# One attention's weights used as fp32 instead of a split pair, in a two-block kernel on one core

## The chip, the core and the metric

The kernel runs on one core of a Trainium2 chip. The core has a matrix engine (TensorE, PE in the profile), a vector engine (VectorE, DVE), an activation engine (ScalarE, ACT), a general engine (GpSimd, POOL) and a queue engine that only starts transfers here (SyncE, SP). Each works through its own list of instructions in order, and they meet through semaphores. The metric is the device time of one execution in microseconds.

## The reference

Sixteen images of 32 x 32 pixels and 128 channels go through two blocks, all in fp32:

```
perceived = depthwise 3x3 conv(x)              # 3 maps per channel
h   = x + up2(gelu(up1(perceived)))            # 128 -> 384 -> 256 -> 128 channels
y   = h + local_attention(h)                   # 3x3 window, softmax over 9
xn  = group_norm(y, 8 groups)
s   = (xn Wq + bq) (xn Wk + bk)^T * scale      # 1024 x 1024 per image
out = xn + (softmax(s) (xn Wv + bv)) Wp + bp
```

The change touches the last product, softmax(s) times the values.

## The kernel before, in words

An image is 1024 pixels, or eight tiles of 128 queries (`TILES`). Most products on TensorE are made of fp32r operands split in two: ScalarE rounds an operand to a high part, a second engine subtracts to get the low part, and `mm3` (L571 to L578) issues three matmuls, high by low, low by high and high by high (L576, L577, L578).

The program is software-pipelined over images by hand. Each engine has three lists of calls: `fill_program`, `turn_program(it)` and `drain_program`. `run` executes the fill, one turn for `it` = 1, a hardware loop of turns for `it` = 2 to 12, and the drain: 12 turns in all. In a turn the names are z = it-1, a = it, b = it+1, c = it+2, d = it+3: a turn finishes the last attention of image a, does the local attention and group norm of image b and the convolution of image c. The order of the calls within a list is the order on the engine. The products use four PSUM banks (`work`); `BANK_PLAN`, `FILL_PLAN` and `DRAIN_PLAN` name for each use its bank, and a product waits (`bank_free`) until the previous user of its bank has been read.

The last attention of an image runs like this, for tile t of eight:

- `scores(n, t)`: TensorE writes 128 x 1024 scores into `ps_s` or `ps_t`; `row_max` (VectorE, L1990) takes the maximum, `exp` (ScalarE, L1116) writes the exponentials `e` and their sums; two `e` buffers.
- `turn_e` (VectorE, L1997) transposes 32 x 32 blocks into `turned`; `send` (SP, L433) writes that to memory (`spread`); `fetch` (SP, L448) reads it back in four transfers as tile t of `et_f`, so that keys lie on partitions. `et_f` holds four tiles, t modulo 4, and `fetch` waits until `values` has read the tile that was there.
- `et_hi_tile` (ScalarE, L1121) rounds the tile to `et_hi`; `et_lo_tile` (GpSimd, L1508) subtracts to get `et_lo`.
- The value operand is the turned xn: `vv` (TensorE), `vv_hi_half` (ScalarE, L1108), `vv_lo_half` (VectorE, L1983).
- `values(n, j)` multiplies two tiles at once: eight key tiles with `mm3`, 24 matmuls of 256 columns into one bank. `a_part` (ScalarE, L1127) copies the result, `attended` (TensorE, L704) applies Wv Wp, `output` (VectorE, L2009) scales and adds `r_tok`, which `residual` (GpSimd, L1567 and L1570) makes from `vv_hi + vv_lo` and then `bp_row`.

Other work that the prediction speaks of: the convolution's six products `conv(c, k)`; their combination on VectorE (`sum_and_difference` L1851, `combine` L1858, `combine_own` L1865, `end_row` L1873); `gelu` and `g_hi_part` on ScalarE (L1029, L1034), `g_lo_part` on GpSimd, then `up2(c, 0)` on TensorE; the transform of the next image (`transform_ends` L1762); the moments and the group norm (`channel_moments` L1943, `group_norm` L1959).

Of the kernel before, what the change touches and what calls it, by code (L numbers as in the profile page):

```python
# [31 lines left out]
F32 = mybir.dt.float32  # L32
F32R = mybir.dt.float32r
# [24 lines left out]
class Count:  # L58
# [14 lines left out]
    ("vv", 1, 0, 1), ("pv", 3, -1, 2), ("pj", 1, -1, 2), ("conv", 0, 2, 0), ("at", 1, 1, 2), ("as", 3, 1, 3),  # L73
    ("conv", 1, 2, 3), ("conv", 2, 2, 1), ("conv", 3, 2, 2), ("at", 2, 1, 3), ("conv", 4, 2, 1), ("at", 3, 1, 2),
# [5 lines left out]
]  # L80
FILL_PLAN = [
    ("conv", 0, 0, 2), ("conv", 1, 0, 0), ("conv", 2, 0, 1), ("conv", 3, 0, 3), ("conv", 4, 0, 2), ("conv", 5, 0, 0),
    ("conv", 0, 1, 3), ("conv", 1, 1, 1), ("conv", 2, 1, 3), ("conv", 3, 1, 0), ("up2", 0, 0, 1), ("conv", 4, 1, 3),
# [15 lines left out]
    ("pv", 3, 12, 2), ("as", 3, 14, 1), ("vv", 1, 13, 2), ("pj", 1, 12, 0), ("conv", 0, 15, 3), ("conv", 1, 15, 0),  # L99
    ("conv", 2, 15, 2), ("conv", 3, 15, 3), ("at", 1, 14, 0), ("conv", 4, 15, 2), ("at", 2, 14, 3),  # L100
# [48 lines left out]
def conv_seq_kernel(nc, ins, out):  # L149
    ctx = ExitStack()  # L150
    with ctx:
# [13 lines left out]
        def placed(name, shape, offset, dt=F32):  # L165
# [65 lines left out]
        vv_at = region("vv_mem", 2 * TILES * 128)  # L231
        vv_hi, vv_lo = (placed(f"vv_{p}", [128, TILES, 128], vv_at + 4 * TILES * 128 * k, F32R)
                        for k, p in enumerate(("hi", "lo")))
# [8 lines left out]
        et_hi, et_lo = (placed(f"et_{p}", [128, 4, 4, TILES, 32], et_at + 4 * TILES * HALF * k, F32R)  # L242
                        for k, p in enumerate(("hi", "lo")))
        et_f = placed("et_f", [128, 4, 4, TILES, 32], et_at + 4 * TILES * HALF)
# [23 lines left out]
        def score_tile(n, t):  # L268
# [32 lines left out]
        vv_hi_ready, vv_lo_ready = count("vv_hi_ready", 2), count("vv_lo_ready", 2)  # L301
        v_sum_ready, r_tok_ready = count("v_sum_ready", 2), count("r_tok_ready", 2)
        max1_ready, e_ready, e_turned, et_hi_ready, et_lo_ready = (
            count("max1_ready", 8), count("e_ready", 8), count("e_turned", 8), count("et_hi_ready", 8),
            count("et_lo_ready", 8))
# [20 lines left out]
                        vv=vv_lo_ready, pv=a_ready, pj=o_ready)  # L326
# [80 lines left out]
        def _(sp):  # L407
# [28 lines left out]
            def fetch(n, t):  # L436

                landed, read = e_sent[t % 2].after(n, t // 2), pe["pv"].after(n, t // 2 - 2)
# [8 lines left out]
                for i in range(4):  # L447
                    sp.dma_start(et_f[32 * i:32 * (i + 1), t % 4].rearrange("r s k q -> r s (k q)"),  # L448
                                 spread[t % 4, :, i].rearrange("(s r) c -> r s c", s=4)) \
                      .then_inc(e_fetched[t % 4].handle, 16)  # L450
# [6 lines left out]
            def fill_program():  # L457
                load_x(1)
                load_x(2)
                send(0, 0)  # L460
                load_x(3)
# [5 lines left out]
                send(0, 4)  # L467
                fetch(0, 2)
                fetch(0, 3)
                send(0, 5)  # L470
                fetch(0, 4)
                fetch(0, 5)

# [3 lines left out]
            def turn_program(it):  # L477
                z, a, d = it - 1, it, it + 3
                send(z, 6)
# [3 lines left out]
                store(z, 0)  # L483
                load_x(d)
                send(a, 0)
                send(a, 2)
                send(a, 1)
                fetch(a, 0)
                fetch(a, 2)
                store(z, 1)  # L490
                fetch(a, 1)
                send(a, 3)
                fetch(a, 3)
                send(a, 5)
# [1885 lines left out]
```

## Time and profile before

| | |
|---|---|
| median of 3 runs | 1090.01 us (1089.63 to 1095.34) |
| profiled execution, own time | 1094.47 us |
| its span, first to last instruction | 1092.7 us |
| mean granted TensorE clock | 0.961 |
| busy: PE, DVE, ACT, POOL | 959.8, 924.5, 727.5, 716.3 us |

A busy share says how long an engine had an instruction in flight, not how long it was needed. Matmuls overlap, so their durations do not add up; the distance between two starts is what one costs in a stream. A wait is put down to the instruction that released it. The granted clock of a stretch is given as a share of 2.4 GHz.

### The profile page before, as it was taken

The numbers are of one execution on the slowest core, as the hardware profiler recorded it, in microseconds if no ns is written. First come the engines' busy times: TensorE is split into PE (matmuls) and PEld (weight loads), VectorE is DVE, ScalarE is ACT, GpSimd is POOL, SyncE is SP. The second block draws the span as 40 slices with busy tenths as digits, with TensorE's granted clock in tenths as the row PEclk, the third lists the DMA queues.
The fourth block names the chain that finished last, engine by engine and source line by source line (L and its number), as shares of the span: only waits on it lengthen the run. The fifth ranks groups of instructions, "written<-read, shape, count | busy, mean of one in ns | idle before, by whom it ended". The sixth has DMA issues, their size and how long they took to land.

```text
span 1092.7 us, 20391 instructions
## 1 busy us (share of the span) xinstructions
PE 959.8 (88%) x6036; PEld 862.8 (79%) x6036; DVE 924.5 (85%) x1628; ACT 727.5 (67%) x1379; POOL 716.3 (66%) x493
## 2 busy tenths in 40 slices
PE   5979898998888999888898988899888898989885
PEld 4968788787787888778797787888778788878775
DVE  6768898888989888898988889888898988987771
ACT  3466876676757767676666767767676676777662
POOL 3644685867667676776767566676775867665665
PEclk9999999999999999999999999999999999999897
DMA  5103465653655546355653655556355554545774
GB/s 89 21 1 85 134 159 169 155 150 101 173 161 123 153 151 169 103 142 168 141 163 115 147 159 126 144 158 169 96 153 164 134 163 132 149 144 154 209 232 138
DMA packets 177654, 152.88 MB, mean 140 GB/s; under 512 B 77776, under 2 KB 161104, under 8 KB 177616
## 3 DMA queue, kind: packets, MB, share of 16 engines
q1 hardware_dynamic: 176768, 152.03, 51.3%
q10 hardware_dynamic: 848, 0.39, 0.2%
q8 instruction: 19, 0.31, 0.1%
q14 instruction: 19, 0.16, 0.0%
HBM read 76.87 MB, written 75.50 MB: 139 GB/s over the span
## 4 chain that ended last, share of the span: by engine, by line
PE 45%; issue 15%; DVE 15%; POOL 4%; DMA 3%; SPq 2%; ACT 1%; DVEq 0%; ACTq 0%; POOLq 0%
PE work L576 9%; PE work L578 9%; PE work L577 9%; DVE turned L1997 3%; PE work L635 2%; DMA spread<-turned 2%; SPq L448 2%; PE ps_s L576 2%; PE work L669 2%; DVE nm L1990 2%; POOL et_lo L1508 2%; DVE gn L1959 2%; PE ps_t L576 2%; PE ps_t L577 2%; PE ps_t L578 2%
## 5 line engine op out<-in xcount | busy, mean ns | idle before, releaser
L1508 POOL TENSOR_TENSOR et_lo<-et_f,et_hi 128x1024 fp32r<-128x1024 f32 x128 | 319.2, 2501 | 129.5 <-ACT et_hi L1121 129.4
L1121 ACT ACTIVATE et_hi<-et_f 128x1024 fp32r<-128x1024 f32 x128 | 135.0, 1057 | 130.5 <-DMA et_f<-spread 130.5
L576 PE MATMUL work<-et_lo,vv_hi 128*128 128x256 f32 x512 | 158.4, 309 | 41.0 <-DVE u L1873 32.9
L576 PE MATMUL work<-t_lo,wc_hi 128*128 128x256 f32 x576 | 166.8, 290 | 0.0
L578 PE MATMUL work<-t_hi,wc_hi 128*128 128x256 f32 x576 | 162.6, 282 | 0.0
L577 PE MATMUL work<-t_hi,wc_lo 128*128 128x256 f32 x576 | 162.3, 282 | 0.0
L1997 DVE STREAM_TRANSPOSE turned<-e 128x1024 f32<-128x1024 f32 x128 | 154.0, 1227 | 9.7 <-ACT e L1116 6.8
L577 PE MATMUL work<-et_hi,vv_lo 128*128 128x256 f32 x512 | 155.4, 303 | 0.0
L578 PE MATMUL work<-et_hi,vv_hi 128*128 128x256 f32 x512 | 154.5, 302 | 0.0
L576 PEld LDWEIGHTS work<-et_lo,vv_hi 128*128 128x128 f32 x512 | 106.0, 207 | 44.4 <-DVE u L1873 31.6
L1508 POOL TENSOR_TENSOR g_lo<-u,g_hi 128x512 fp32r<-128x512 f32 x60 | 76.3, 1293 | 84.3 <-ACT g_hi L1034 84.3
L1508 POOL TENSOR_TENSOR t_lo<-t_f,t_hi 128x512 fp32r<-128x512 f32 x48 | 63.6, 1326 | 73.6 <-ACT t_hi L1008 73.2
L576 PEld LDWEIGHTS work<-t_lo,wc_hi 128*128 128x128 f32 x576 | 109.5, 190 | 2.0
L577 PEld LDWEIGHTS work<-t_hi,wc_lo 128*128 128x128 f32 x576 | 109.8, 191 | 0.7
L578 PEld LDWEIGHTS work<-t_hi,wc_hi 128*128 128x128 f32 x576 | 109.1, 189 | 0.0
L578 PEld LDWEIGHTS work<-et_hi,vv_hi 128*128 128x128 f32 x512 | 107.4, 210 | 0.0
L577 PEld LDWEIGHTS work<-et_hi,vv_lo 128*128 128x128 f32 x512 | 106.1, 207 | 0.6
L1990 DVE TENSOR_REDUCE nm<-ps_t 128x1 f32<-128x1024 f32 x64 | 77.8, 1216 | 10.0 <-PE ps_t L578 10.0
L1116 ACT ACTIVATE e<-ps_s,nm 128x1024 f32<-128x1024 f32 x64 | 71.2, 1112 | 20.5 <-DVE nm L1990 19.9
L576 PE MATMUL ps_s<-kk_lo,qq_hi 128*128 128x512 f32 x128 | 55.5, 433 | 28.3 <-ACT e L1116 28.3
L1990 DVE TENSOR_REDUCE nm<-ps_s 128x1 f32<-128x1024 f32 x64 | 77.7, 1214 | 2.6 <-PE ps_s L578 2.2
L1116 ACT ACTIVATE e<-ps_t,nm 128x1024 f32<-128x1024 f32 x64 | 70.9, 1108 | 3.5 <-DVE nm L1990 3.4
(181 smaller groups left out, 2680.7 us busy)
## 6 DMA issues: line engine op xcount, KB each, us to landing
spread<-turned SPq DMA_DIRECT2D x128, 512.0 KB, 3.0
et_f<-spread SPq DMA_DIRECT2D x512, 128.0 KB, 3.5
x_in<-in_x SPq DMA_DIRECT2D x64, 128.0 KB, 4.2
out<-r_tok SPq DMA_DIRECT2D x32, 256.0 KB, 3.7
w_up_t<-in_L_conv_w_up SPq DMA_DIRECT2D x1, 384.0 KB, 4.1
y<-in_L_conv_w_qkv SPq DMA_DIRECT2D x1, 192.0 KB, 4.7
const<-in_const ACTq DMA_DIRECT2D x1, 166.0 KB, 5.1
y<-in_L_conv_w_up ACTq DMA_DIRECT2D x1, 128.0 KB, 4.9
```

What stands on the lines that cost most here:

```text
L448: sp.dma_start(et_f[32 * i:32 * (i + 1), t % 4].rearrange("r s k q -> r s (k q)"), spread[t % 4, :, i].rearrange("(s r) c -> r s c", s=4)) \
L576: te.matmul(dst, wh, xl, start=first, stop=False)
L577: te.matmul(dst, wl, xh, start=False, stop=False)
L578: return te.matmul(dst, wh, xh, start=False, stop=last)
L635: mm = te.matmul(bank("v", half, n)[:, t * 128:(t + 1) * 128], h[:, pix], wv0[:, :], start=True, stop=True)
L669: te.matmul(dst[:, u * 128 - before:(u + 1) * 128 + behind], v_pix[:, t, :], pt[half][:, at - before:at + 128 + behind], start=(u == 0), s ...
L1116: act.activation(e_both[:, t % 2], score_tile(n, t)[:, :], ACT.Exp, bias=nm1[:, t:t + 1], accum_out=sum1[:, t:t + 1]) \
L1121: act.activation(et_hi[:, t % 4].rearrange("p s k q -> p (s k q)"), et_f[:, t % 4].rearrange("p s k q -> p (s k q)"), ACT.Copy).then_inc(e ...
L1508: return pool.tensor_tensor(dst, full, hi, ALU.subtract)
L1959: dve.tensor_tensor(gn_a, gamma, rstd, ALU.mult).then_inc(gn_step.handle, 1)
L1990: dve.tensor_reduce(nm1[:, t:t + 1], score_tile(n, t)[:, :], AX.X, ALU.max, negate=True) \
L1997: dve.transpose(turned_both[:, t % 2].rearrange("p i k q -> p k i q"), e_both[:, t % 2].rearrange("p (k i q) -> p k i q", k=TILES, i=4)).t ...
```

## The change

- `et_hi`, `et_lo` and `et_f` become one fp32 tensor `et` of eight tiles, in the same space. `fetch` lands tile t in place t and waits for the product of the image before (`pv` of n - 1) instead of the product two steps back.
- `values` issues eight plain fp32 matmuls of 256 columns instead of 24 fp32r ones, and waits for the transfers themselves. `et_hi_tile` and `et_lo_tile` are gone: 128 ScalarE and 128 GpSimd instructions of 128 x 1024.
- The value operand is a plain copy `vv_c`; `vv_lo_half` is gone, and `residual` is one addition instead of two.
- The calls of all five lists are in another order, and the bank plans go with it.

```diff
-        et_hi, et_lo = (placed(f"et_{p}", [128, 4, 4, TILES, 32], et_at + 4 * TILES * HALF * k, F32R)
-                        for k, p in enumerate(("hi", "lo")))
-        et_f = placed("et_f", [128, 4, 4, TILES, 32], et_at + 4 * TILES * HALF)
+        et = placed("et", [128, TILES, 4, TILES, 32], et_at)
...
-                landed, read = e_sent[t % 2].after(n, t // 2), pe["pv"].after(n, t // 2 - 2)
+                landed, read = e_sent[t % 2].after(n, t // 2), pe["pv"].after(n - 1, t // 2)
...
-                two = slice(2 * (j % 2), 2 * (j % 2) + 2)
-                te.wait_ge(*et_lo_ready.after(n, 2 * j + 1))
-                te.wait_ge(*vv_lo_ready.after(n, 1))
+                for t in (2 * j, 2 * j + 1):
+                    te.wait_ge(*e_fetched[t % 4].after(n, t // 4))
+                te.wait_ge(*vv_ready.after(n, 1))
                 te.wait_ge(*bank_free("pv", j, n))
                 for kt in range(TILES):
-                    mm = mm3(bank("pv", j, n)[:, 0:256], (vv_hi[:, kt, :], vv_lo[:, kt, :]),
-                             [x[:, two, :, kt, :].rearrange("p t s q -> p (t s) q") for x in (et_hi, et_lo)],
-                             kt == 0, kt == TILES - 1)
+                    mm = te.matmul(bank("pv", j, n)[:, 0:256], vv_c[:, kt, :],
+                                   et[:, 2 * j:2 * j + 2, :, kt, :].rearrange("p t s q -> p (t s) q"),
+                                   start=(kt == 0), stop=(kt == TILES - 1))
...
-            def et_hi_tile(n, t):
-                act.wait_ge(*e_fetched[t % 4].after(n, t // 4))
-                act.activation(et_hi[:, t % 4].rearrange("p s k q -> p (s k q)"),
-                               et_f[:, t % 4].rearrange("p s k q -> p (s k q)"), ACT.Copy).then_inc(et_hi_ready.handle, 1)
...
-            def et_lo_tile(n, t):
-                pool.wait_ge(*et_hi_ready.after(n, t))
-                minus(et_lo[:, t % 4].rearrange("p s k q -> p (s k q)"), et_f[:, t % 4].rearrange("p s k q -> p (s k q)"),
-                      et_hi[:, t % 4].rearrange("p s k q -> p (s k q)").bitcast(F32)).then_inc(et_lo_ready.handle, 1)
...
-                pool.tensor_tensor(r_tok[:, :, :], vv_hi[:, four, :].bitcast(F32), vv_lo[:, four, :].bitcast(F32), ALU.add) \
-                    .then_inc(v_sum_ready.handle, 1)
-                pool.wait_ge(*v_sum_ready.after(n, k))
-                pool.tensor_tensor(r_tok[:, :, :], r_tok[:, :, :], bp_row[:, :].rearrange("p (a c) -> p a c", a=1)
+                pool.tensor_tensor(r_tok[:, :, :], vv_c[:, four, :], bp_row[:, :].rearrange("p (a c) -> p a c", a=1)
...
-    ("vv", 1, 0, 1), ("pv", 3, -1, 2), ("pj", 1, -1, 2), ("conv", 0, 2, 0), ("at", 1, 1, 2), ("as", 3, 1, 3),
+    ("as", 2, 1, 2), ("as", 3, 1, 3), ("at", 0, 1, 1), ("conv", 0, 2, 0), ("at", 1, 1, 1), ("vv", 0, 0, 2),
```

The order moves at three places that matter here. The first is TensorE in a turn from the end of `values(a, 0)` (`et_lo`, `vv_hi`), over the second half of the local values (`pt,v_pix`, image b), to the half product `up2` (`g_lo`, `w_hi`, image c). Before:

```order
L578 MATMUL work<-et_hi,vv_hi 128x256
L664 REGISTER_ALU
L669 MATMUL work<-pt,v_pix 128x160
L669 MATMUL work<-pt,v_pix 128x192 x2
L669 MATMUL work<-pt,v_pix 128x160
L672 MATMUL work<-pt,v_pix 128x32
L595 ISA
L596 REGISTER_ALU
L576 MATMUL work<-g_lo,w_hi 128x512
```

After:

```order
L667 MATMUL work<-pt,v_pix 128x160
L670 MATMUL work<-pt,v_pix 128x32
L721 ISA
L723 REGISTER_ALU
L725 MATMUL work<-et_61,vv_c_60 128x256 x8
L674 ISA
L678 MATMUL work<-moments,const 128x2
L593 ISA
L594 REGISTER_ALU
L574 MATMUL work<-g_lo_52,w2_hi 128x512
```

Between the local values and `up2(c, 0)` there now stand `values(a, 0)`, as eight matmuls, and the group's moments; before, `values(a, 0)` came ahead of the local values and `up2` right behind them. Ahead of the rows shown after, `scores(a, 6)` has moved up to follow the last convolution product.

The second place is ScalarE around the gelus (`u` is the hidden map, `e` the exponentials), before:

```order
L1116 ACTIVATE e,sum<-ps_t,nm 128x1024
L1026 ISA
L1029 ACT_TABLE_LOAD
L1029 ACTIVATE u<-u,cols 128x512 x2
L1032 ISA
L1034 ACTIVATE g_hi<-u 128x512
L1032 REGISTER_ALU
L1034 ACTIVATE g_hi<-u 128x512
L1082 ACTIVATE pt<-work 128x2x128
L1029 ACTIVATE u<-u,cols 128x512 x2
```

and after:

```order
L1030 ACT_TABLE_LOAD
L1030 ACTIVATE u<-u,cols 128x512 x2
L1033 ISA
L1035 ACTIVATE g_hi<-u 128x512
L1113 REGISTER_ALU
L1117 ACT_TABLE_LOAD
L1117 ACTIVATE e,sum<-ps_t,nm 128x1024
L1033 REGISTER_ALU
L1035 ACTIVATE g_hi<-u 128x512
L1030 ACT_TABLE_LOAD
L1030 ACTIVATE u<-u,cols 128x512
```

An exponential, `exp(a, 5)`, now stands between the first and the second `g_hi`, and with it two more table loads in a turn.

The third is GpSimd, from the start of the looped turn, before:

```order
L1508 TENSOR_TENSOR et_lo<-et_f,et_hi 128x1024
L1561 ISA
L1562 REGISTER_ALU
L1567 TENSOR_TENSOR r_tok<-vv_hi,vv_lo 128x512
L1570 TENSOR_TENSOR r_tok<-r_tok,bp_row 128x512
L1555 REGISTER_ALU
L1508 TENSOR_TENSOR et_lo<-et_f,et_hi 128x1024
L1555 REGISTER_ALU
L1508 TENSOR_TENSOR et_lo<-et_f,et_hi 128x1024
L1534 ISA
L1508 TENSOR_TENSOR g_lo<-u,g_hi 128x512
```

and after:

```order
L1467 TENSOR_TENSOR xn_lo<-y,xn_hi 128x512
L1500 ISA
L1467 TENSOR_TENSOR h_lo<-h,h_hi 128x512
L1480 REGISTER_ALU
L1481 ISA
L1483 TENSOR_TENSOR t_f<-d_54 128x8x32
L1484 TENSOR_TENSOR t_f<-d_54 128x8x32
L1471 ISA
L1473 TENSOR_TENSOR d_53<-xp 128x256 x4
```

The eight `et_lo` subtractions of a turn are gone; the transform of the image to be convolved stands at the turn's start, and the `g_lo` parts have no large subtraction ahead of them.

## Rows read from the trace of the kernel before

**Rows 1.** Busy time by stretch: stretch, length, busy of PE, PEld, DVE, ACT, POOL, PEclk, DMA

```profile
267.40:918.60 651.20, 582.51 (x3742) 526.85 (x3742) 579.30 (x1001) 448.64 (x851) 445.15 (x301) 0.97 0.54 145
```

**Rows 2.** One line's instructions, 206 to 964 us: count, minimum, median, maximum ns, starts

```profile
L1959 DVE TENSOR_TENSOR gn<-cols,gn x11: 2220/2228/2234, 267.3 to 918.5; 128x1 f32<-128x1 f32 x11
```

**Rows 3.** Waits of PE, 267.4 to 918.6 us: total us, times, longest

```profile
PE work L576 <- DVE u L1873: 27.9, 10, 3.2
PE ps_s L576 <- ACT e L1116: 20.9, 10, 2.1
PE work L635 <- DVE r_tok L2009: 11.0, 10, 1.3
PE work L680 <- DVE moments L1943: 7.6, 10, 0.8
```

**Rows 4.** Instructions in order of time, DVE and POOL: start us, duration us, line

```profile
503.10 3.49 DVE L1858 SCALAR_TENSOR_TENSOR u<-u 128x512 f32<-128x512 f32 x2
...
503.15 5.65 POOL L1508 TENSOR_TENSOR et_lo<-et_f,et_hi 128x1024 fp32r<-128x1024 f32 x2 [0.23 <-ACT et_hi L1121]
```

**Rows 5.** As rows 2 for VectorE's lines (the last: over the whole run)

```profile
L1858 DVE SCALAR_TENSOR_TENSOR u<-u x24: 692/2844/2945, 243.5 to 960.5; 128x512 f32<-128x512 f32 x24
...
L1762 DVE SCALAR_TENSOR_TENSOR t_f<-d x24: 657/1747/2804, 215.9 to 932.8; 128x256 f32<-128x256 f32 x24
...
L1959 DVE TENSOR_TENSOR gn<-cols,gn x16: 148/2227/2342, 84.1 to 1029.6; 128x1 f32<-128x1 f32 x16
```

**Rows 6.** Matmuls of PE in order of time

```profile
510.84 0.28 PE L577 MATMUL work<-et_hi,vv_lo 128*128 128x256 f32 x1
510.95 0.28 PE L578 MATMUL work<-et_hi,vv_hi 128*128 128x256 f32 x1
...
515.09 1.35 PE L669 MATMUL work<-pt,v_pix 128*128 128x160 f32 x8
...
517.89 0.39 PE L576 MATMUL ps_s<-kk_lo,qq_hi 128*128 128x512 f32 x1
518.12 0.39 PE L577 MATMUL ps_s<-kk_hi,qq_lo 128*128 128x512 f32 x1
...
543.66 1.54 PE L648 MATMUL work<-kp,q_c 128*128 128x204 f32 x8
```

**Rows 7.** As rows 1, two stretches of one turn

```profile
507.90:511.40 3.50, 0.79 (x6) 0.79 (x7) 3.50 (x5) 3.47 (x5) 0.91 (x1) 1.00 0.00 0
511.40:514.80 3.40, 3.40 (x18) 3.40 (x17) 3.29 (x6) 3.40 (x7) 1.59 (x2) 0.51 0.16 64
```

**Rows 8.** Groups by line and shape, whole run: count, busy us, mean ns, idle before

```profile
L1508 POOL TENSOR_TENSOR et_lo<-et_f,et_hi 128x1024 fp32r<-128x1024 f32 x128 | 319.2, 2501 | 129.5 <-ACT et_hi L1121 129.4
...
L1121 ACT ACTIVATE et_hi<-et_f 128x1024 fp32r<-128x1024 f32 x128 | 135.0, 1057 | 130.5 <-DMA et_f<-spread 130.5
...
L1983 DVE TENSOR_TENSOR vv_lo<-work,vv_hi 128x512 fp32r<-128x512 f32 x32 | 21.4, 672 | 8.8 <-ACT vv_hi L1108 8.8
...
L1029 ACT ACT_TABLE_LOAD x16 | 20.5, 1283 | 0.3
```

**Rows 9.** Instructions in order of time, ACT and POOL around the gelus

```profile
508.77 1.10 ACT L1116 ACTIVATE e<-ps_t,nm 128x1024 f32<-128x1024 f32 x1
...
511.27 1.34 ACT L1029 ACTIVATE u<-u,cols 128x512 f32<-128x512 f32 x2
512.51 1.13 ACT L1034 ACTIVATE g_hi<-u 128x512 fp32r<-128x512 f32 x2
...
513.20 2.53 POOL L1508 TENSOR_TENSOR g_lo<-u,g_hi 128x512 fp32r<-128x512 f32 x2 [4.40 <-ACT g_hi L1034]
```

**Rows 10.** Instructions in order of time, the end of the last image

```profile
1077.48 0.58 PE L576 MATMUL work<-et_lo,vv_hi 128*128 128x256 f32 x1 [4.28 <-POOL et_lo L1508]
...
1079.74 1.06 ACT L1121 ACTIVATE et_hi<-et_f 128x1024 fp32r<-128x1024 f32 x1 [0.62 <-DMA et_f<-spread]
...
1083.92 0.39 PE L576 MATMUL work<-et_lo,vv_hi 128*128 128x256 f32 x1 [1.55 <-POOL et_lo L1508]
```

More of the change, by code:

```diff
@@ L781, in fill_program @@
                 local_scores(0, 2)
+                v(0, 0)
                 local_scores(0, 3)
@@ L784, in fill_program @@
                 up2(1, 0)
+                v(0, 1)
                 local_probs_t(0, 1)
+                local_probs_t(0, 2)
                 local_values(0, 0)
-                local_probs_t(0, 2)
                 local_probs_t(0, 3)
                 local_values(0, 1)
-                v(1, 0)
+                up2(1, 1)
+                k(1, 0)
                 group_moments(0)
                 q(1, 0)
-                up2(1, 1)
+                v(1, 0)
+                v(1, 1)
                 vv(0, 0)
-                k(1, 0)
-                v(1, 1)
+                vv(0, 1)
+                k(1, 1)
                 qq(0, 0)
@@ L843, in fill_program @@
                 v(2, 1)
+                scores(1, 0)
+                k(2, 1)
+                scores(1, 1)
                 local_scores(2, 0)
-                scores(1, 0)
-                scores(1, 1)
+                values(0, 2)
+                q(2, 1)
                 local_scores(2, 1)
-                local_scores(2, 2)
-                values(0, 2)
-                vv(1, 0)
-                local_probs_t(2, 0)
                 scores(1, 2)
-                scores(1, 3)
             def turn_program(it):
@@ L859, in turn_program @@
                 z, a, b, c = it - 1, it, it + 1, it + 2
+                local_scores(b, 2)
+                local_scores(b, 3)
+                scores(a, 3)
+                local_probs_t(b, 0)
+                conv(c, 0)
+                local_probs_t(b, 1)
+                vv(a, 0)
+                conv(c, 1)
+                values(z, 3)
+                local_probs_t(b, 2)
                 vv(a, 1)
-                values(z, 3)
                 scores(a, 4)
                 attended(z, 1)
-                conv(c, 0)
@@ L894, in turn_program @@
+                kk(b, 0)
+                qq(b, 0)
+                kk(b, 1)
+                v(c, 1)
+                values(a, 2)
                 k(c, 1)
                 q(c, 1)
-                vv(b, 0)
-                local_scores(c, 0)
                 scores(b, 0)
                 scores(b, 1)
+                qq(b, 1)
+                local_scores(c, 0)
                 local_scores(c, 1)
-                local_scores(c, 2)
                 scores(b, 2)
-                scores(b, 3)
-                local_probs_t(c, 0)
@@ L909, in drain_program @@
             def drain_program():
+                scores(B - 3, 3)
+                local_scores(B - 2, 2)
+                conv(B - 1, 0)
+                local_probs_t(B - 2, 0)
+                local_scores(B - 2, 3)
                 values(B - 4, 3)
-                local_scores(B - 2, 3)
-                vv(B - 3, 1)
+                vv(B - 3, 0)
                 scores(B - 3, 4)
+                conv(B - 1, 1)
+                local_probs_t(B - 2, 1)
                 attended(B - 4, 1)
                 scores(B - 3, 5)
-                conv(B - 1, 0)
@@ L941, in drain_program @@
-                k(B - 1, 1)
-                scores(B - 2, 0)
-                scores(B - 2, 1)
+                up2(B - 1, 1)
+                attended(B - 3, 0)
+                qq(B - 2, 0)
+                qq(B - 2, 1)
+                values(B - 3, 2)
+                k(B - 1, 1)
+                kk(B - 2, 0)
+                kk(B - 2, 1)
                 local_scores(B - 1, 0)
                 local_scores(B - 1, 1)
-                v(B - 1, 0)
+                scores(B - 2, 0)
                 q(B - 1, 1)
+                scores(B - 2, 1)
@@ L948, in drain_program @@
+                local_probs_t(B - 1, 0)
+                local_scores(B - 1, 2)
+                local_scores(B - 1, 3)
                 scores(B - 2, 2)
                 scores(B - 2, 3)
-                local_scores(B - 1, 2)
-                values(B - 3, 2)
-                local_probs_t(B - 1, 0)
-                scores(B - 2, 4)
-                values(B - 3, 3)
-                local_scores(B - 1, 3)
-                attended(B - 3, 1)
                 local_probs_t(B - 1, 1)
                 v(B - 1, 1)
+                values(B - 3, 3)
@@ L959, in drain_program @@
+                scores(B - 2, 4)
+                local_probs_t(B - 1, 2)
+                scores(B - 2, 5)
+                local_probs_t(B - 1, 3)
                 vv(B - 2, 0)
-                scores(B - 2, 5)
                 vv(B - 2, 1)
-                local_probs_t(B - 1, 2)
+                attended(B - 3, 1)
+                local_values(B - 1, 0)
+                local_values(B - 1, 1)
                 scores(B - 2, 6)
-                local_values(B - 1, 0)
-                local_probs_t(B - 1, 3)
@@ L1979, in kk_lo_half @@
                     .then_inc(kk_lo_ready.handle, 1)
-            def vv_lo_half(n, k):
-                dve.wait_ge(*vv_hi_ready.after(n, k))
-                dve.tensor_tensor(vv_lo[:, 4 * k:4 * k + 4, :], bank("vv", k, n)[:, :].rearrange("p (t c) -> p t c", t=4),
-                                  vv_hi[:, 4 * k:4 * k + 4, :].bitcast(F32), ALU.subtract) \
-                   .then_inc(vv_lo_ready.handle, 1)
             def row_max(n, t):
```

868 lines of the change are left out of this document (376 added, 492 removed), and 54 rows, old and new, of tables (BANK_PLAN, DRAIN_PLAN, FILL_PLAN).

## The prediction

> **What bounds the kernel now.** I read the views in this order: busy time over ten whole turns, the length of a turn, TensorE's waits, what stretches VectorE's instructions, the price of each kind of matmul, and the end of the last image.
>
> A turn takes 65.1 us: the group norm's line starts at 267.3 and, ten turns later, at 918.5 [rows 2]. In a turn PE is busy 58.3 us, VectorE 57.9, ScalarE 44.9 and GpSimd 44.5 [rows 1]. Two engines are nearly full, so shares alone don't say which sets the pace. TensorE's waits do: in the same stretch it waited 27.9 us for the convolution's sums on VectorE, 20.9 for exponentials, 11.0 for an output and 7.6 for the moments, ten times each [rows 3]. That is 6.7 us a turn, which with 58.3 makes the turn. The reader is to see that three of the four releasers are VectorE and that the fourth, the exponential, itself waits for VectorE's row maxima. The kernel is TensorE waiting for VectorE.
>
> VectorE in turn is held up. Its `combine` at 503.10 needs 3.49 us for two instructions, while GpSimd runs `et_lo` from 503.15 [rows 4]. The same instruction takes 0.69 us at its shortest and 2.84 at the median; the transform's line takes 0.66 and 1.75; the group norm's 128 x 1 operation takes 0.15 us at the start and end of the program and 2.23 in the turns [rows 5]. With `combine_own`, which is stretched in the same way, I estimate 9 us of VectorE's 57.9 as standing behind GpSimd, nearly all of it behind the 2.5 us subtractions.
>
> There is a third loss. After a stretch of 3.5 us in which PE was busy for 0.79, the granted clock is 0.51, the lower level of 1.2 GHz, for 3.4 us [rows 7]. Over the turns the clock is 0.97 [rows 1], so about 0.03 x 65.1 = 1.95 us a turn go to it.
>
> **The change part by part.**
>
> *The product on TensorE, dearer.* A split matmul of 256 columns costs 0.115 to 0.12 us in the stream (510.84 to 510.95) [rows 6]; a `values` call is 24 x 0.118 = 2.83 us. Plain fp32 of 256 columns is not in the trace; the nearest row is the local scores, plain fp32 of 204 columns: each matmul shows as two records, and eight records take 1.54 us [rows 6]. The last record's length is about 0.34, so one costs (1.54 - 0.34) / 7 = 0.172 us, or 0.84 ns a column. For 256 columns that is 0.216, and 16 records are 3.45 us. So a call costs 0.62 us more, a turn 2.5, all 64 calls 40. Bounds: 3.3 us a call if part of the 0.172 is a fixed cost; 3.7 if each of four passes costs per column what the split scores cost, 0.23 us for 512 (517.89 to 518.12) [rows 6]. I take 3.45, from the nearer row. All of it lies on TensorE, which sets the end.
> The Trainium skill ("FP8 and Floating Point Precision", TensorE Precision Notes) says that true FP32 makes 4 passes through the array, and it speaks against this change, as the split makes three. By that ratio alone a call would be 4/3 x 2.83 = 3.77 us, the turn 1.3 us longer than by the rows and the time some 15 us higher.
>
> *The rounding and the subtraction, gone.* ScalarE loses 135.0 us, GpSimd 319.2, VectorE (`vv_lo`) 21.4 [rows 8]; one of `residual`'s two additions goes as well. That is 8.4, 20 and 1.3 us a turn. ScalarE and GpSimd had 20 us idle in a turn, so by themselves these are worth nothing. What counts is what stood behind them. VectorE's instructions are no longer held for 2 us at a time. GpSimd keeps subtractions of half the size, 1.27 us each (two `g_lo` in 2.53) [rows 9], and these can still hold VectorE. VectorE falls from 57.9 to about 49 us a turn and stops being full.
>
> *Eight tiles, and waits on the transfers.* `values` now waits for the fetch itself. Ahead of it a conversion of 1.06 and a subtraction of 2.5 us disappear. The fetches may start earlier, because the place is free since the last image; their number and bytes are the same, and DMA engines are 0.54 busy [rows 1]. I cost this at nothing in the turns.
>
> *The new order.* I followed each engine's list by hand through one turn with the durations above; the result is an estimate. TensorE's own work is 58.3 - 1.95 (clock) + 2.5 = 58.8 us as busy time. Four waits remain. The largest is at `up2(c, 0)`. From the last convolution product it takes about 0.25 to reach VectorE, 0.5 until VectorE is there, 0.69 for `end_row`, then on ScalarE 1.34 for two gelus, 0.57 for a `g_hi`, a table load of 1.28 and an exponential of 1.3 with its sum, 0.57 for the second `g_hi`, and 1.27 for `g_lo` [rows 8, 9]; with the steps between engines 8.0 us. TensorE has in that time `scores(a, 6)` at 6 x 0.23, the local values at 1.3, `values(a, 0)` at 3.45 and the moments at 0.3 [rows 6]: 6.5 us. It waits 1.5, where it waited 2.8 before. The exponential between the gelus costs two table loads that nothing needs, 2.6 us of ScalarE, and it is what keeps this wait alive. The other three are waits for a bank or a scaled probability at the turn's start (`values(z, 3)` for a bank that ScalarE empties seventh in its turn, `local_probs_t(b, 3)` for the output, `local_probs_t(b, 0)`): 0.95, 0.35 and 0.2 us. Together 3.0. Some 0.25 of each is the running-out of the matmul before, already in the busy time, so about 2.0 is added: 60.8. For what GpSimd's remaining instructions still do to VectorE I add 0.5 (bounds 0 and 2.7). The waits are shorter than those after which the clock fell, so I put that loss at 0 (upper bound 1.95). **A turn of 61.3 us.**
>
> *The sum.* Twelve turns: 12 x (65.1 - 61.3) = 46 us. The end of the last image: the last fetch lands at 1079.7, where ScalarE starts on it; the product starts at 1083.92 and runs until 1086.8 [rows 10]. Now it starts at 1079.8 and takes 3.45: 3.6 us earlier. Before it, the wait of 4.28 us for `et_lo` [rows 10] shrinks to one for the transfer. Against that stand twelve dearer calls in the drain, partly under those waits; I take 5 for the drain (bounds 0 and 13). The start-up has little attention in it: 0, give or take 5. The sum is 51. The profiled execution took 1094.5 and would take 1043; the median of the runs shown is 1090, so **1039 us**.
>
> **The rivals.**
>
> *TensorE pays and the waits stay: 1122.* If the four waits are set by chains that GpSimd did not stretch, they stay at 6.7 us and the turn is 65.1 + 2.5 = 67.6: 12 x 2.5 = 30, with 2 for the drain, over 1090. It decides from the point at which the waits shrink by less than 2.5 us a turn. For it speaks the new exponential between the gelus. Against it: the stretched `combine` and the group norm's operation stand in the very chains that end three of the waits. 6 in 100.
>
> *GpSimd's small subtractions hold VectorE instead: 1066.* Five of VectorE's instructions with two operands in the on-chip memory (two transform ends, moments, group variance, group norm) can each meet one of 1.27 us. If 2.7 of these 6 us reach TensorE the turn is 63.5: 12 x 1.6 = 19, and 5 for the drain. For it: `combine` could be held by half-size instructions as well. Against it: in the new list nothing is due on GpSimd while `combine` runs.
> The Trainium skill ("SBUF — State Buffer", Who interferes with whom, and the two sides before it) states this as an exclusive lock for the whole instruction: what starts second waits until the first has ended. The trace agrees: the 2.84 us of `combine` are its 0.69 plus most of a 2.5 us subtraction. 20 in 100, of which 4 end within half a per cent.
>
> *TensorE never waits: 1004.* The turn is its own 58.8 us: 12 x 6.3 = 76, and 10 for the drain. 10 in 100.
>
> **How the numbers follow.** The forecast has 64 in 100. A measurement of this kernel can tell 0.5%, or 5.4 us, from no change. Faster by more: 0.64 + 0.10 + 0.16 = 0.90; same: 0.04; slower: 0.06. Low end: the third rival's 1004. High end: a turn of 63.3 with the clock's loss left, 0 for the drain and 5 for the start-up: 1090 - 22 + 5 = 1073, which holds most of the second rival too. Outside lie the first rival and a few of each other case.
>
> **What would show it.** Right: a turn between 60 and 62.5 us; TensorE's two records of a plain 256-column matmul 0.21 to 0.22 us apart; `combine` near 0.7 us at the median and the group norm's operation below 1; waits for the convolution's sums gone from the top, and a wait of some 1.5 us a turn at `up2` for `g_lo`. Wrong: VectorE still above 55 us a turn; `values` waiting for fetches; a record above 0.25 us; or a granted clock below 0.95 in the turns, which would mean that the remaining waits cost twice.

## The result and the profile after

The changed kernel takes 1001.2 us (median of 4 runs, 999.7 to 1001.8) where the kernel before takes 1089.8 (four runs as well; the 1090.0 ahead of the prediction is of three): a ratio of 0.917 with a 95% interval of 0.914 to 0.920. It saves 88.6 us, and 51 were forecast: the direction was right, the size wrong, and the time lies 3 us below the low end of the range. The profiled execution took 1001.8 us with a span of 999.9. One of the four executions of the run old_order below took 3369 us; its figures here are those of the other three (1013.8 to 1015.5).

The busy time by stretch of the changed kernel: ten turns, counted from the start of the group norm's line in one turn to that ten turns later, and the drain (columns as in [rows 1]).

```profile
251.43:839.20 587.77, 580.15 (x3421) 516.22 (x3420) 471.93 (x981) 390.42 (x791) 211.73 (x201) 1.00 0.57 161
839.20:999.90 160.70, 145.75 (x766) 124.64 (x764) 113.87 (x223) 81.77 (x174) 34.89 (x32) 0.98 0.66 188
```

Ten turns take 587.8 us where they took 651.2 [rows 1, 2]: a turn is 58.8 us, not 65.1. TensorE is busy for 58.0 of it, VectorE for 47.2 (57.9 before), and the clock is 1.00 instead of 0.97. The stretch of the drain of the kernel before is this:

```profile
918.60:1092.70 174.10, 145.97 (x873) 129.65 (x871) 125.55 (x226) 110.37 (x201) 108.77 (x65) 0.92 0.58 170
```

So the 92.8 us between the two spans (1092.7 and 999.9) are made up of 74.2 in the twelve turns from the group norm's second start to its fourteenth (780.0 us before, 705.8 after), 13.5 in the drain and 5.1 in the start-up. (The drain is counted from the fourteenth start, 918.46 before and 839.20 after; the window above begins 0.14 us later.)

What TensorE still waits for in those ten turns, as [rows 3] (total us, times, longest), is one line of any size; 6.7 us a turn have become 0.7:

```profile
PE work L574 <- POOL g_lo L1467: 7.1, 10, 0.8
```

VectorE's groups by line and shape in the same ten turns (count, busy us, mean ns, idle before), which answer to [rows 5]:

```profile
L1772 DVE SCALAR_TENSOR_TENSOR u<-u 128x512 f32<-128x512 f32 x20 | 12.9, 688 | 0.3
...
L1676 DVE SCALAR_TENSOR_TENSOR t_f<-d 128x256 f32<-128x256 f32 x20 | 11.6, 671 | 0.0
...
L1873 DVE TENSOR_TENSOR gn<-cols,gn 128x1 f32<-128x1 f32 x10 | 5.4, 541 | 0.0
```

`combine` is at 688 ns on average, where 692 was its shortest before [rows 5]; the transform's line and the group norm's operation have fallen as well.

The plain product in order of time on TensorE (start, duration): 16 records start at 514.04, and the next matmul starts at 517.49.

```profile
514.04 3.62 PE L725 MATMUL work<-et,vv_c 128*128 128x256 f32 x16
517.49 0.38 PE L655 MATMUL work<-const,pn 128*128 128x128 f32 x2
```

That is 3.45 us a call, 0.216 a record, as worked out from the local scores in [rows 6]. The estimate of 3.77 us, four thirds of the split call by the four passes that the Trainium skill's "FP8 and Floating Point Precision" (TensorE Precision Notes) states for true FP32, is not what the trace shows.

### The profile page after: what moved, and what is told of

The parts are those of the page before. It is cut to its first block, busy times and chain, and to the rows that moved or that the text cites. A ratio compares the mean times of both kernels' runs of the same rounds, so it can differ in the third digit from the quotient of the medians.

```text
span 999.9 us, 18992 instructions
## 1 busy us (share of the span) xinstructions
PE 954.9 (95%) x5524; PEld 845.9 (85%) x5524; DVE 775.7 (78%) x1596; ACT 626.3 (63%) x1275; POOL 345.2 (35%) x333
## 4 chain that ended last, share of the span: by engine, by line
PE 40%; issue 36%; POOL 11%; DVE 7%; DMA 2%; ACT 1%; SPq 1%; DVEq 0%; POOLq 0%; ACTq 0%
PE work L725 10%; PE work L574 6%; PE work L575 5%; PE work L576 5%; POOL t_lo L1467 3%; POOL g_lo L1467 3%; POOL d L1473 3%; DVE turned L1905 2%; PE work L702 2%; PE work L633 2%; PE work L667 1%; POOL r_tok L1521 1%; DVE xp L1651 1%; PE ps_t L575 1%; PE ps_t L574 1%
## 5 line engine op out<-in xcount | busy, mean ns | idle before, releaser
L725 PE MATMUL work<-et,vv_c 128*128 128x256 f32 x1024 | 235.3, 383 | 8.9 <-issue 8.8
L725 PEld LDWEIGHTS work<-et,vv_c 128*128 128x128 f32 x1024 | 191.4, 191 | 35.6 <-issue 11.2
L1030 ACT ACTIVATE u<-u,cols 128x512 f32<-128x512 f32 x60 | 41.2, 715 | 70.3 <-DVE u L1787 70.1
L1123 ACT ACTIVATE a_c<-work 128x256 f32<-128x256 f32 x64 | 23.2, 384 | 82.1 <-PE work L725 82.0
L1917 DVE SCALAR_TENSOR_TENSOR r_tok<-work,rec,r_tok 128x128 f32<-128x128 f32 x128 | 36.1, 345 | 46.8 <-issue 29.3
L1074 ACT ACTIVATE pn<-p,rec 128x192 f32<-128x192 f32 x128 | 51.1, 448 | 21.8 <-PE work L655 13.2
L1065 ACT ACTIVATE p<-p,nm 128x204 f32<-128x204 f32 x128 | 57.7, 458 | 1.4 <-DVE nm L1822 1.4
L1521 POOL TENSOR_TENSOR r_tok<-vv_c,bp_row 128x512 f32<-128x512 f32 x32 | 41.1, 1285 | 49.2 <-DMA out<-r_tok 49.2
L1467 POOL TENSOR_TENSOR h_lo<-h,h_hi 128x512 fp32r<-128x512 f32 x32 | 40.7, 1273 | 49.2 <-ACT h_hi L1042 49.1
```

Of the source, the lines that this page charges most:

```text
L725: mm = te.matmul(bank("pv", j, n)[:, 0:256], vv_c[:, kt, :], et[:, 2 * j:2 * j + 2, :, kt, :].rearrange("p t s q -> p (t s) q"), start=(kt ...
L1030: act.activation(u_half(n, k), u_half(n, k), ACT.Gelu, bias=b_hid[:, m:m + 1]).then_inc(g_ready.handle, 1)
L1065: ins_ = act.activation(tile, tile, ACT.Exp, bias=nm0[:, t:t + 1], scale=-1.0, accum_out=sum0[:, t:t + 1])
L1074: ins_ = act.activation(pn[:, u, :].rearrange("p (r w) -> p r w", r=6), p0[:, 2 * (j % 2) + u, :, 1:1 + W], ACT.Copy, scale=rec0[:, t:t + 1])
L1467: return pool.tensor_tensor(dst, full, hi, ALU.subtract)
L1521: pool.tensor_tensor(r_tok[:, :, :], vv_c[:, four, :], bp_row[:, :].rearrange("p (a c) -> p a c", a=1) .broadcast_to([128, 4, 128]), ALU.a ...
```

## Experiments

Turns are ten-turn differences of the group norm's starts; "longest" is TensorE's longest wait in them.

| run | time, us | ratio to before (95%) | turn | PE busy a turn | clock | longest |
|---|---|---|---|---|---|---|
| before | 1089.8 | | 65.1 | 58.3 | 0.97 | 3.2 |
| changed | 1001.2 | 0.914 to 0.920 | 58.8 | 58.0 | 1.00 | 0.8 |
| no_et_lo | 1060.1 | 0.968 to 0.974 | 63.2 | 58.4 | 0.96 | 3.2 |
| no_et_hi | 1120.9 | 1.026 to 1.032 | 67.9 | 59.4 | 0.95 | 4.8 |
| old_order | 1014.0 | 0.925 to 0.933 | 60.1 | 58.2 | 1.00 | 0.8 |
| round_back | 1065.6 | 0.974 to 0.978 | 63.6 | 59.5 | 0.98 | 2.2 |
| sub_at_combine | 1017.8 | 0.930 to 0.938 | 60.1 | 58.2 | 0.99 | 1.9 |
| fill_at_combine | 1001.8 | 0.915 to 0.921 | 58.8 | 58.0 | 1.00 | 0.8 |
| four_tiles | 1001.4 | 0.916 to 0.920 | 58.8 | 58.0 | 1.00 | 0.8 |
| short_values | 989.7 | 0.905 to 0.910 | 58.2 | 55.0 | 1.00 | 1.7 |
| exp_early | 990.7 | 0.907 to 0.911 | 57.9 | 57.9 | 1.00 | none |
| exp_early_short | 970.3 | 0.886 to 0.891 | 56.5 | 54.9 | 1.00 | 0.8 |

**GpSimd's subtraction alone (no_et_lo).** The kernel before, with this on TensorE and without the calls of `et_lo_tile`:

```diff
-                te.wait_ge(*et_lo_ready.after(n, 2 * j + 1))
+                te.wait_ge(*et_hi_ready.after(n, 2 * j + 1))
...
-                             [x[:, two, :, kt, :].rearrange("p t s q -> p (t s) q") for x in (et_hi, et_lo)],
+                             [x[:, two, :, kt, :].rearrange("p t s q -> p (t s) q") for x in (et_hi, et_hi)],
```

> The kernel before, in its own call order and with the split product, but GpSimd's subtraction et_lo is not issued: the product reads et_hi in the place of et_lo, so the low part of the exponentials is left out. TensorE's work is the same as before. Theory A (TensorE waited for VectorE, and VectorE stood behind GpSimd's 2.5 us subtractions): combine falls from 2.84 to about 0.7 us, the group norm's operation from 2.2 to below 1, VectorE from 57.9 to about 49 us a turn, the waits for the convolution's sums nearly vanish, and the turn falls from 65.1 to 58 to 60.5 us: 1005 to 1035 us. Theory B (the new call order and bank plan removed the waits): the turn stays above 63.5, the time above 1070 us.

On VectorE it went as theory A says; of the time 29.7 us went, where theory A wanted 55 at least and theory B under 20. VectorE's groups in ten turns:

```profile
L1813 DVE SCALAR_TENSOR_TENSOR u<-u 128x512 f32<-128x512 f32 x20 | 12.9, 688 | 0.3
...
L1914 DVE TENSOR_TENSOR gn<-cols,gn 128x1 f32<-128x1 f32 x10 | 1.2, 118 | 0.0
```

`combine` is free again and the waits for the convolution's sums are gone. But the turn falls by only 1.9 us. The waits of TensorE, then of ScalarE, in the same ten turns:

```profile
PE work L669 <- ACT pt L1082: 29.1, 10, 3.2
PE work L680 <- DVE moments L1898: 6.2, 10, 0.8
```
```profile
ACT et_hi L1121 <- DMA et_f<-spread: 49.1, 37, 2.8
```

A new wait of 2.9 us a turn stands where the old one was: the local values wait for the probabilities `pt`, which ScalarE copies out of their bank. ScalarE in order of time shows why (in brackets, the idle time before and what ended it):

```profile
430.66 1.06 ACT L1121 ACTIVATE et_hi<-et_f 128x1024 fp32r<-128x1024 f32 x1 [1.90 <-DMA et_f<-spread]
...
436.00 1.06 ACT L1121 ACTIVATE et_hi<-et_f 128x1024 fp32r<-128x1024 f32 x1 [2.37 <-DMA et_f<-spread]
...
439.47 1.33 ACT L1029 ACTIVATE u<-u,cols 128x512 f32<-128x512 f32 x2
...
441.75 0.36 ACT L1082 ACTIVATE pt<-work 128x256 f32<-128x256 f32 x1
```

`et_hi` stands twice for a transfer, and the exponential, the gelus and `pt` stand behind it in ScalarE's list. ScalarE is idle in these gaps, and nothing behind them can use them.

**Everything removed, the old order (old_order).** The kernel before with `values`, `vv_half`, `fetch`, `residual` and the eight tiles of the change; of its lists only the removed calls are missing:

```diff
-                et_hi_tile(a, 0)
                 pt_pair(b, 1)
                 take(c, 0, 1)
                 take(c, 2, 3)
-                et_hi_tile(a, 1)
```

> The plain product and all removals, eight tiles held, but the call orders and bank plans of the kernel before (only the removed calls are missing from the lists). Theory A: the turn is that of the run without et_lo plus at most 2.5 us for the dearer product: 60 to 62.5 us, 1025 to 1055 us; what is left to the 1001 us of the changed kernel is the new order's. Theory B: the waits stay and the dearer product comes on top, a turn of 66 to 67.6 us: 1100 to 1122 us.

1014.0 us, 11 under what theory A allows, though the turn of 60.1 us lies in its range; theory B, that the order did it, falls. Of the 88.6 us, 75.8 come without any new order, although the product is dearer, and 12.8 are the new order's. The turn is now even 3.1 us shorter than without `et_lo` alone, though TensorE has 2.5 more to do. Of what else went, `et_hi` is the suspect, and the next run puts its place back.

**The rounding's wait, put back (round_back).** In the kernel of old_order, at each old place of `et_hi_tile`:

```diff
+            def round_tile(n, t):
+                act.wait_ge(*e_fetched[t % 4].after(n, t // 4))
+                act.wait_ge(*rounded.after(n, t - 2))
+                act.activation(scratch[:, t % 2, :], wc_hi[:, 0:3].rearrange("p n t d -> p (n t d)")[:, 0:1024].bitcast(F32),
+                               ACT.Copy).then_inc(rounded.handle, 1)
```

> The run in the old call order with the plain product, and on ScalarE, at each place of its list where et_hi stood, one conversion of 128 x 1024 again that waits for the same transfer; it reads a constant, writes a scratch that nobody reads, and nobody waits for it. Theory C (the conversions were not free: they stood in ScalarE's list waiting for transfers, and the local probabilities queued behind them): TensorE's wait at the local values for the turned probabilities is back at 2 to 3 us a turn, the turn goes from 60.1 to 62.5 to 65 us, 1044 to 1075 us. Rival (ScalarE has 23 us idle in a turn, so they cost nothing, as the forecast put it): 60.1 us, 1012 to 1018 us.

1065.6 us, 52 more than without it, and the wait is back at 2.1 us a turn. ScalarE's waits for it, then TensorE's, in ten turns:

```profile
ACT scratch L1173 <- DMA et<-spread: 48.1, 34, 2.7
```
```profile
PE work L665 <- ACT pt L1078: 20.9, 10, 2.2
```

Nobody reads what these conversions write, and ScalarE has 19 us idle in a turn even so. ScalarE in order of time, two conversions ahead of the `pt` that TensorE waits for:

```profile
432.92 1.06 ACT L1173 ACTIVATE scratch<-wc_hi 128x1024 f32<-128x1024 f32 x1 [1.42 <-DMA et<-spread]
...
438.58 1.06 ACT L1173 ACTIVATE scratch<-wc_hi 128x1024 f32<-128x1024 f32 x1 [2.69 <-DMA et<-spread]
```

From the start of the second half of `take` (the copy that stands ahead of these conversions) to the end of this `pt`, ScalarE takes 13.8 us here and 10.3 in old_order. Three conversions in it are 3.0 us of work and 4.1 of waiting for transfers; old_order has 3.6 us of idle time in the same place, which would have held the work but not the wait. By these rows it is mainly the wait at the head of the list that costs; a run with conversions that wait for nothing was not made. TensorE's busy time grew by 1.3 of the 3.5 us a turn, at the same number of matmuls and a clock of 0.98 instead of 1.00.

**The rounding alone removed (no_et_hi).** The kernel before without `et_hi_tile`; GpSimd waits for the transfer itself:

```diff
-                pool.wait_ge(*et_hi_ready.after(n, t))
+                pool.wait_ge(*e_fetched[t % 4].after(n, t // 4))
...
-                             [x[:, two, :, kt, :].rearrange("p t s q -> p (t s) q") for x in (et_hi, et_lo)],
+                             [x[:, two, :, kt, :].rearrange("p t s q -> p (t s) q") for x in (et_lo, et_lo)],
```

> The kernel before, in its own call order and with the split product, but ScalarE's rounding et_hi is not issued; GpSimd's subtraction et_lo stays, as long as before: it waits for the transfer itself and subtracts a constant, and the product reads its result in both places, so the exponentials are not split. In the run without et_lo ScalarE stood 49.1 us in ten turns in front of et_hi for a transfer, and the local probabilities queued behind it were what TensorE waited for (29.1). Theory C (two queues each hold TensorE: VectorE behind GpSimd's subtraction, and ScalarE's list behind et_hi's waits for transfers; with either left the turn stays long): combine stays near 2.8 us, the waits for the convolution's sums stay at 2 to 3 us a turn, the turn is 62.5 to 64.5 us, 1060 to 1085 us. Theory A (the subtraction alone): 65 us and 1090. Rival (et_hi's waits alone are what it took): below 61.5 us, under 1050.

1120.9 us: slower than before, outside what any of the three theories gave. The subtractions now start without ScalarE, and so elsewhere in VectorE's list. GpSimd, VectorE and TensorE in order of time:

```profile
548.73 2.38 POOL L1463 TENSOR_TENSOR et_lo<-et_f,wc_hi 128x1024 fp32r<-128x1024 f32 x1 [0.83 <-DMA et_f<-spread]
...
553.03 2.59 POOL L1463 TENSOR_TENSOR et_lo<-et_f,wc_hi 128x1024 fp32r<-128x1024 f32 x1
```
```profile
549.13 3.48 DVE L1709 SCALAR_TENSOR_TENSOR t_f<-d 128x256 f32<-128x256 f32 x2
552.45 3.65 DVE L1718 SCALAR_TENSOR_TENSOR t_f<-d 128x256 f32<-128x256 f32 x2
```
```profile
559.17 0.80 PE L576 MATMUL ps_s<-kk_lo,qq_hi 128*128 128x512 f32 x1 [4.84 <-ACT e L1116]
```

Both pairs of transform instructions of VectorE now stand beside an `et_lo`. The second pair did so before as well, the first did not; before they were:

```profile
540.02 1.10 DVE L1753 SCALAR_TENSOR_TENSOR t_f<-d 128x256 f32<-128x256 f32 x2
540.95 3.29 DVE L1762 SCALAR_TENSOR_TENSOR t_f<-d 128x256 f32<-128x256 f32 x2
```

Behind them stand the local mask, the row maxima and so the exponential, for which TensorE waits 4.84 us, 46.2 in ten turns where it was 20.9 [rows 3]. So the two removals are no sum: one alone gives 30 us, the other alone loses 31, both together with a dearer product give 76.

**The hold at combine, alone (sub_at_combine, fill_at_combine).** In the changed kernel one call `hold(c)` behind `residual(z, 1)` in GpSimd's turn; in the second run two memsets stand in the place of its last two lines:

```diff
+            def hold(n):
+                pool.wait_ge(*u_step.after(n, 2))
+                pool.tensor_tensor(scratch[:, 1024:1025], bp_row[:, 0:1], bp_row[:, 0:1], ALU.subtract)
+                row = bp_row[:, :].rearrange("p (a c) -> p a c", a=1).broadcast_to([128, 8, 128])
+                pool.tensor_tensor(scratch[:, 0:1024].rearrange("p (a c) -> p a c", a=8), row, row, ALU.subtract)
```
```diff
+                for k in range(2):
+                    pool.memset(scratch[:, 1149 * k:1149 * (k + 1)], 0.0)
```

> The changed kernel, and in each of the twelve turns one more subtraction on GpSimd, 128 x 1024 fp32 with both operands in the on-chip memory, whose result nobody reads. It waits for the first of the two instructions ahead of combine, so that it has just begun when combine is due, and GpSimd is idle there until g_lo. Theory A (a subtraction on GpSimd holds VectorE's instructions with two operands in the on-chip memory until it ends): the first combine takes about 2.5 us instead of 0.69, everything behind it comes 1.9 us later, the wait at up2 for g_lo grows from 0.7 to about 2.6 us, the turn from 58.8 to 60.2 to 60.8: 1018 to 1026 us. Rival (GpSimd's work off the chain costs nothing): 1001 us, combine at 0.69.

> As the run with the subtraction at combine, but in its place two memsets of 128 x 1149, about 2 us together, which write the on-chip memory and read nothing. If what holds VectorE is GpSimd's reading, as the subtraction does: combine stays at 0.69 and the time at 1001 us, within 3. If any work of GpSimd on the on-chip memory holds it: combine at about 2.2 us, 1013 to 1022 us.

The subtraction in order of time, and `combine` beside it:

```profile
473.76 1.90 POOL L1541 TENSOR_TENSOR scratch<-bp_row 128x1024 f32<-128x1024 f32 x1
```
```profile
474.17 2.64 DVE L1780 SCALAR_TENSOR_TENSOR u<-u 128x512 f32<-128x512 f32 x2
```

It ran until 475.66, beside the pair of `combine`, which took 2.64 us, 1.35 more than free; over the ten turns the mean of one is 1358 ns where it is 688 in the changed kernel. TensorE's wait for `g_lo` grew by 1.1 us a turn (18.0 in ten turns), the turn by 1.3, the time by 16.5. That is theory A with a shorter hold than I put in: this subtraction, both operands the same row, takes 1.90 and not 2.5 us. The memsets in the same place, and `combine` with them:

```profile
468.33 2.05 POOL L1541 MEMSET scratch<- 128x1149 f32 x2
```
```profile
L1780 DVE SCALAR_TENSOR_TENSOR u<-u 128x512 f32<-128x512 f32 x20 | 12.9, 688 | 0.3
```

They change nothing: 1001.8 us. So it is not the time that GpSimd is busy, but its reading of the on-chip memory, that holds VectorE here.

**Four tiles instead of eight (four_tiles).** The changed kernel with the room and the wait of before:

```diff
-                landed, read = e_sent[t % 2].after(n, t // 2), pe["pv"].after(n - 1, t // 2)
+                landed, read = e_sent[t % 2].after(n, t // 2), pe["pv"].after(n, t // 2 - 2)
```

> The changed kernel with four tiles of the exponentials held instead of eight, so that a fetch waits for the product two calls back and not for that of the image before. By my costing at nothing (the fetches come later than those products anyway): 1001 us, within 3, and no waits for fetches on TensorE. Rival (the room lets the fetches start earlier and that is part of the gain): a turn longer by 0.5 us or more, above 1007 us.

1001.4 us, and the same single wait. The eight tiles are worth nothing here, as forecast.

**Is TensorE alone the bound? (short_values, exp_early, exp_early_short)** Two edits of the changed kernel, and both together:

```diff
-                for kt in range(TILES):
+                for kt in range(6):
```
```diff
                 exp(a, 4)
+                exp(a, 5)
                 gelu(c, 0)
                 gelu(c, 1)
                 g_hi_part(c, 0)
-                exp(a, 5)
```

> The changed kernel with six of the eight blocks of keys in the last product; the two last blocks are left out of the weighted sum. A call is 12 records instead of 16, 2.59 instead of 3.45 us, a turn has 3.45 us less work on TensorE. Theory A (TensorE alone sets the pace now, one to one): the turn falls from 58.8 to 55.3 to 55.8, and with the calls of the drain the time to 950 to 960 us. Rival (a chain through VectorE, ScalarE or GpSimd is close behind): the turn stays above 57, the time above 980 us, and the wait at up2 grows by what the product was shortened by.

With 16 records of 0.216 us less on TensorE a turn, 3.45 us, the turn fell by only 0.6, and the time by 11.5: the rival holds. TensorE's waits in ten turns:

```profile
PE work L574 <- POOL g_lo L1467: 16.4, 10, 1.7
PE work L574 <- ACT a_c L1123: 7.1, 9, 0.8
PE work L655 <- DVE r_tok L1917: 4.4, 10, 0.4
PE work L574 <- DVE kk_lo L1801: 4.1, 10, 0.4
```

Of the 2.5 us a turn of waiting that came back, 0.9 stand at `up2` for `g_lo`, as much as one call was shortened by, and 1.6 at three other places. So the product's length covers several chains of nearly the same length. The plain product is dearer by 0.62 us a call, 2.5 a turn; since even 3.45 us less a turn gains only 0.6, most of that costs nothing in this order: TensorE would wait instead.

> The changed kernel with one call moved: on ScalarE the exponential of tile 5 goes ahead of the first gelu instead of between g_hi of the first and of the second half. ScalarE is idle there (5.6 us before the gelus), and two of the table loads of a turn go. Theory A (TensorE's only wait left, 0.7 us a turn for g_lo at up2, hangs on this exponential): the wait vanishes, the turn falls from 58.8 to 58.0 to 58.2, 991 to 995 us. Rival (something else is late next at the same place, as the moments or a bank): 998 to 1001 us.

990.7 us and a turn of 57.9, just under what theory A gave (991 to 995, 58.0 to 58.2), and the fastest of the kernels that leave nothing out. The busy time of ten turns:

```profile
249.79:828.69 578.90, 578.54 (x3421) 515.53 (x3420) 474.61 (x982) 363.44 (x771) 211.76 (x201) 1.00 0.59 163
```

TensorE is busy for 578.5 of 578.9 us. What the exponential did between the gelus in the changed kernel, ScalarE in order of time:

```profile
534.44 0.61 ACT L1035 ACTIVATE g_hi<-u 128x512 fp32r<-128x512 f32 x1
535.07 1.28 ACT L1117 ACT_TABLE_LOAD   x1
536.37 1.11 ACT L1117 ACTIVATE e<-ps_t,nm 128x1024 f32<-128x1024 f32 x1
537.38 0.19 ACT L1117 ACTIVATION_READ_ACCUMULATOR e<-ps_t,nm 128x1 f32 x1
537.47 0.62 ACT L1035 ACTIVATE g_hi<-u 128x512 fp32r<-128x512 f32 x1
538.11 1.28 ACT L1030 ACT_TABLE_LOAD   x1
```

One load and the exponential, 2.4 us, stand ahead of the second `g_hi`, for which `g_lo` and `up2` wait.

> The run with the exponential ahead of the gelus, and in it six of the eight blocks of keys in the last product (the two last blocks are left out of the weighted sum): 3.45 us less work on TensorE a turn. With the product shortened alone the turn fell by 0.55 us, and 1.64 us of new and old wait stood at up2 for g_lo, 0.71 for a_c, 0.44 for an output and 0.41 for kk_lo. Theory A (the convolution's chain to up2, with the exponential in it, is what the product's length covers): the wait for g_lo goes, the others stay, 1.6 us: the turn is 56 to 56.6 us, 965 to 975 us. Rival (the next chain takes its place at the same length): the turn stays above 57.3 us, the time above 980.

970.3 us, a turn of 56.5: the wait for `g_lo` is gone, and 0.79 a turn for `a_c`, 0.43 for an output and 0.41 for `kk_lo` are left, as expected. With the chain out of the way, 1.4 of the 3.45 us come through instead of 0.6; the next waits are worth 1.6 us.

## Why the prediction was wrong in size

*What bounds the kernel before: half right.* That TensorE waited for VectorE, and VectorE stood behind GpSimd, is shown: without `et_lo` `combine` fell to 688 ns and the waits for the convolution's sums went, and one subtraction put at `combine` in the changed kernel made TensorE wait 1.1 us a turn more. Not seen was the second queue. I read [rows 3], which name what ended last, and took ScalarE's conversions for idle-time work. Under VectorE's lateness lay ScalarE's, from `et_hi` waiting for transfers at the head of its list.

*"The rounding and the subtraction, gone ... by themselves these are worth nothing": the step that failed in kind.* I counted ScalarE's work against its 20 us of idle time. The same amount of work with the same waits, put back alone (round_back), costs 52 us. [rows 8] held the warning: 130.5 us of idle time before `et_hi`, ended by transfers. For each engine one has to ask what is queued behind a waiting instruction; I asked it for GpSimd only. The forecast's turn did not hang on it, as I walked through the new lists, which don't hold these conversions; what made the number wrong are the terms below.

*The product: right.* 3.45 us a call, 0.216 a record. That "all of it lies on TensorE, which sets the end" was only half so, as short_values shows.

*The turn of 61.3 us: the terms that were mis-sized.* Measured 58.8, 2.5 less: 0.8 in TensorE's own work, 1.24 in the waits and 0.5 in GpSimd's small subtractions. Of the 41.8 us by which the spans' difference of 92.8 exceeds the 51 of the sum, the twelve turns are 28.2 (74.2 instead of 46). The waits: 2.0 was added for four, and 0.76 is what ten turns have beside busy time, 1.24 less. The wait at `up2` is 0.7, not 1.5: I put the chain at 8.0 us, and from the last convolution matmul's end at 532.35 to the end of `g_lo` at 539.44 it is 7.1. Most of the difference is the 0.5 us that I gave VectorE to get there: it was already waiting, and starts at 532.48. The wait at `values(z, 3)`, put at 0.95, isn't there: ScalarE emptied the bank at 513.76, and the product starts at 514.04. Nor are the two smaller ones. GpSimd's small subtractions: 0.5 was added, and nothing of it shows on TensorE; VectorE's 128 x 1 operations still meet them (541 ns for the group norm's, where 118 ns are free), but TensorE does not wait for them. TensorE's own work: 58.8 was put, 58.0 measured. I took 58.3, subtracted the clock and left in it the running-out of matmuls ahead of all waits of before; in exp_early, which has no waits, it is 57.9. That this running-out makes up the 0.8 is the likeliest reading, but no run separates it from the clock's share. So the rival "TensorE never waits", with its 58.8 us a turn, hit the measured turn by luck, from two terms that were each off by 0.8: own work 58.8 and no wait, where 58.0 and 0.76 were measured.

*Drain and start-up: mis-sized.* 13.5 us, not 5, in the drain, and 5.1, not 0, in the start-up. Removing `et_lo` alone shortens the drain to 162.5 us, removing everything in the old order to 159.1. TensorE's busy time in it is the same before and after (146 us), dearer calls and all, and its clock rose from 0.92 to 0.98: most of the waits went, as in the turns. What is left of them is mainly ahead of the product, 8.1 us in six waits that the view puts down to no instruction; that they are waits for the fetches is likely, and not shown. Both terms lie just outside the bounds that I gave, 13 for the drain and 5 for the start-up; what shortened the start-up was not looked into.

*The rivals.* That the waits stay (1122 us) and that the small subtractions hold VectorE (1066) are both excluded by the trace after. Of the forecast's signs of being right, the record's length, `combine` and the group norm's operation came out; the waits for the convolution's sums went too. The turn did not lie in 60 to 62.5 us, and the wait at `up2` is half of the 1.5 us named; of the signs of being wrong, a product that waits for fetches may have come in the drain, and none came in the turns.

*What stays open.* The clock's share in no_et_lo and round_back wasn't separated from the waits that precede it. Which place of the new order brings its 12.8 us wasn't tried piece by piece; in old_order TensorE still waits 0.77 us a turn for the moments, 0.62 for `qq_lo` and 0.55 for the exponential, 1.9 together, against 0.7 in the changed kernel, and that is most of the 1.3 us between the two turns. What `vv_lo` and the second addition of `residual` were worth wasn't tried by themselves. How far no_et_hi's loss depends on the moment at which the transfers land wasn't tried either.

## What to carry to other kernels

Work that fits into an engine's idle time is free only if it never waits at the head of that engine's list: before costing a removed instruction at nothing, look at the idle time in front of it, what ended that, and what is queued behind. When the longest wait is removed, look for a second chain of nearly the same length under it; a view of waits names only the one that came last. An operation that is dearer on the bounding engine may cost little where that engine would have waited anyway, and moving one call out of a chain may then bring as much as making the operation shorter: 10.5 us for the exponential that moved (exp_early), 11.5 for a product a quarter shorter (short_values).

## What the runs showed of the hardware

A GpSimd subtraction that reads the on-chip memory held a two-operand instruction of VectorE until it ended (the pair 2.64 us instead of 1.29), and memsets of 2.05 us in the same place did not (688 ns each). The Trainium skill ("SBUF — State Buffer", Who interferes with whom) says just this: two inputs contend with a GpSimd instruction that reads, not with one that only writes. These runs agree.

The granted clock of the turns was 1.00 in the runs in which TensorE had no wait or a longest one of 0.8 or 1.7 us, 0.99 with 1.9, 0.98 with 2.2, and 0.95 to 0.97 with 3.2 to 4.8; these runs differ in more than their longest wait. In round_back TensorE waits 2.1 us a turn more than in old_order, and is busy 1.3 us a turn longer with the same 3422 matmuls in ten turns. So a wait removed here gave back more than its own length.

A GpSimd subtraction of 128 x 1024 took 1.90 us with the same 128 columns as both operands (sub_at_combine), and `et_lo`, with two different operands, 2.40 us at the median in the kernel before (2.33 to 2.94). The two also differ in the type that they write, so what makes the difference isn't shown.
